# Skip rows made in the output stage from the destination rows, and source rows normalised by ScalarE

## The reference

```
x = layernorm(x + L0(x))      # attention over the edges: 4 heads of 64, then @ W_out
x = layernorm(x + L1(x))

# L1, for z = the normalised row of a node
m   = z @ W_n2m.T                                  # 128 features
q, k, v  = m @ Wq.T + bq, m @ Wk.T + bk, m @ Wv.T + bv
e   = (edge_attr @ W_edge.T) @ We.T
alpha = softmax over the edges of a destination of q[dst] . (k[src] + e) * scale
agg = segment_sum((v[src] + e) * alpha, dst)       # 128 features
x_r = m @ Wskip.T + bskip                          # the skip row
beta = sigmoid([agg, x_r, agg - x_r] @ Wbeta.T)
L1  = (beta * x_r + (1 - beta) * agg) @ W_m2n.T
```

## Time and profile before

| what | us |
|---|---|
| median of 3 runs | 1362.51 (1362.12 to 1378.24) |
| the profiled execution's own time | 1371.76 |
| its span, first to last instruction | 1370.0 |
| mean granted clock of TensorE | 0.958 |

### The profile page before, as it was taken

How to read it: one execution, slowest core, us unless ns; L and a number is a source line. 1 busy time by engine, 2 the same in 40 slices (tenths; PEclk the granted TensorE clock), 3 DMA queues, 4 the chain that set the end, 5 groups by cost and what they waited for, 6 DMA issues and landing times. The chain is left out here.

```text
span 1370.0 us, 28397 instructions
## 1 busy us (share of the span) xinstructions
PE 1198.5 (87%) x7186; PEld 1044.4 (76%) x7186; DVE 1045.4 (76%) x3775; ACT 808.2 (59%) x2683; POOL 838.7 (61%) x1044
## 2 busy tenths in 40 slices
PE   3799999999996799899898699999999994788881
PEld 2688898988895677777776699999999993566660
DVE  3476676776679798889787788888888877788781
ACT  0366565665567765666556466666666667365562
POOL 4688888888743455455444566666666643267675
PEclk9899999999999999999999899999999998799995
DMA  6668889888763487887777766667666642556541
GB/s 157 196 184 260 261 257 273 269 273 266 233 199 121 142 248 237 242 247 240 221 238 208 221 199 196 199 185 211 197 191 204 195 129 78 161 180 185 174 156 57
DMA packets 208937, 277.05 MB, mean 202 GB/s; under 512 B 40060, under 2 KB 140563, under 8 KB 208777
## 3 DMA queue, kind: packets, MB, share of 16 engines
q1 hardware_dynamic: 188793, 224.13, 53.2%
q0 software_dynamic: 19264, 50.85, 12.9%
q10 hardware_dynamic: 720, 0.26, 0.1%
HBM read 159.73 MB, written 117.12 MB: 202 GB/s over the span
## 5 line engine op out<-in xcount | busy, mean ns | idle before, releaser
L743 PE MATMUL banks<-m_ext,node_XT 128*128 128x257 f32 x1568 | 379.9, 385 | 0.0
L743 PEld LDWEIGHTS banks<-m_ext,node_XT 128*128 128x128 f32 x1568 | 288.2, 194 | 33.7
L769 DVE SCALAR_TENSOR_TENSOR node_X<-banks,node_be,node_X 128x256 f32<-128x256 f32 x392 | 169.8, 475 | 83.9 <-ACT node_be L695 69.8
L670 POOL TENSOR_TENSOR node_r<-node_vv,half 128x4 f32<-128x4 f32 (+1 forms) x202 | 214.6, 1062 | 17.2 <-POOL node_vv L665 0.3
L701 ACT ACTIVATE node_XT<-banks 128x512 f32<-128x512 f32 x196 | 117.1, 598 | 143.7 <-PE banks L733 137.5
L665 POOL TENSOR_SCALAR node_vv<-node_mv 128x4 f32<-128x4 f32 (+1 forms) x202 | 57.6, 285 | 223.7 <-DVE node_mv L777 207.2
L762 DVE BATCH_NORM_STATS2 node_st<-node_X 128x6 f32<-128x256 f32 x392 | 145.8, 414 | 17.4 <-DMA node_X<-in_x 16.1
L708 ACT ACTIVATE node_sq<-node_X 128x256 f32<-128x256 f32 x392 | 157.9, 408 | 0.0
L733 PE MATMUL banks<-ident,node_X 128*128 128x128 f32 x784 | 123.6, 281 | 30.1 <-DVE node_X L783 15.1
L682 ACT ACTIVATE node_X<-node_X,node_r 128x256 f32<-128x256 f32 x326 | 145.9, 496 | 1.4 <-POOL node_r L670 1.4
L733 PEld LDWEIGHTS banks<-ident,node_X 128*128 128x128 f32 x784 | 96.7, 150 | 43.0 <-issue 20.1
(11 more groups left out here) (265 smaller groups left out, 2730.6 us busy)
## 6 DMA issues: line engine op xcount, KB each, us to landing
node_X<-in_x SPq DMA_DIRECT2D x196, 256.0 KB
out<-node_X SPq DMA_DIRECT2D x196, 256.0 KB
ring<-rows SPq DMA_DIRECT2D x210, 128.0 KB
rows<-ring SPq DMA_DIRECT2D x100, 256.0 KB
rows<-ring SPq DMA_DIRECT2D x200, 128.0 KB
MB<-keeps SPq DMA_DIRECT2D x40, 320.0 KB, 5.4
store<-rows SPq DMA_DIRECT2D x90, 128.0 KB
MB<-picks SPq DMA_DIRECT2D x50, 128.0 KB
```

Source lines behind the costliest of these rows:

```text
L670: pool.tensor_tensor(r[:, s % 4, NT * lo:NT * hi], v, self.c.half[:, NT * lo:NT * hi], ALU.pow).then_inc(self.roots, 1)
L743: last = pe.matmul(ps[:, NT * o + k, 0:D + 1], self.XT[:, o, k * D + h * P:k * D + (h + 1) * P], c.m_ext[:, h, :], start=(h == 0), stop=(h ...
L769: last = dve.scalar_tensor_tensor(out=X[:, n % U, k, :], in0=ps[:, b + k, 0:D], scalar=self.be[:, n % 4, k:k + 1], in1=X[:, n % U, k, :], ...
```

## The change

Skip rows: the message stage no longer makes or keeps them. In the output stage TensorE transposes the destination rows that are loaded there anyway, in two halves into bank 6; ScalarE copies them with 1.0 added into `ZT` (four slots); two products with `m_ext` give the skip product and its part of the gate's logit (columns 0 to 256). `w_out1` gets two more columns, plus and minus `wa`, so that the aggregate's product carries the other part of the logit in both signs; ScalarE copies these two numbers out (`part`) and gives them as bias to the two sigmoids. The one-column product falls away. The MSG transposes have bank 5 alone, so each waits for the scan of the tile just before. The loads of rows wait for `made` instead of `product`.

Source rows: VectorE normalises the destination side alone. For the source side it makes minus mean times root for two tiles at once (`nb`), in odd steps, as the first instruction of the step, after a wait for `roots`; ScalarE then scales and shifts the row, between its `ST` copy and its K copy. The waits for `normed` of TensorE and GpSimd are joined by waits for `src_normed`; VectorE's QK waits for the Q product itself.

The diff, cut to its core:

```
 Weights, VectorE, s == 1
-                own(dve.tensor_copy(c.wa[:, :], w.wa))
+                own(dve.tensor_copy(c.w_out1[:, D + 1:D + 2], w.wa))
+                own(dve.tensor_scalar(c.w_out1[:, D + 2:D + 3], w.wa, -1.0, None, ALU.mult))
 Message, GpSimd
                 at_least(pool, self.normed, 2 * g - 4)
+                at_least(pool, self.src_normed, 2 * g - 4)
 Message, TensorE
                 pe.wait_ge(self.normed, t + 1)
+                pe.wait_ge(self.src_normed, t + 1)
...
-                at_least(pe, self.x_kept, n)
                 at_least(pe, self.q_used, n)
-                for h in range(2):
-                    pe.matmul(ps[:, 7, DM:2 * DM], c.w_qs[:, h, DM:2 * DM], c.ST[:, o, (2 + h) * P:(3 + h) * P], start=(h == 0), stop=(h == 1))
 Message, ScalarE, after the ST copy
+            if live(t, -1, TILES):
+                n = t + 1
+                g = n // 2
+                k = 2 * (n % 2) + 1
+                act.wait_ge(self.shifted, g + 1)
+                row = c.ring[:, n % c.R, 1, :]
+                act.activation(row, row, ACT.Identity, bias=self.nb[:, g % 3, n % 2:n % 2 + 1], scale=self.r[:, g % 3, k:k + 1]).then_inc(self.src_normed, 1)
...
-                act.wait_ge(self.q_product, n + 1)
-                act.activation(c.store[:, n, DM:2 * DM], ps[:, 7, DM:2 * DM], ACT.Copy).then_inc(self.x_kept, 1)
 Message, VectorE, first in the step
+            if t % 2 == 1 and live(t, -1, TILES):
+                g = (t + 1) // 2
+                dve.wait_ge(self.roots, g + 1)
+                at_least(dve, self.src_normed, 2 * g - 4)
+                dve.scalar_tensor_tensor(out=self.nb[:, g % 3, :], in0=self.mv[:, g % 3, :, 1, 0], scalar=-1.0,
+                                         in1=self.r[:, g % 3, :].rearrange("p (k s) -> p k s", s=2)[:, :, 1], op0=ALU.mult, op1=ALU.mult).then_inc(self.shifted, 1)
...
-                dve.wait_ge(self.x_kept, n + 1)
+                dve.wait_ge(self.q_product, n + 1)
...
-                for side in range(2):
-                    k = 2 * (n % 2) + side
-                    row = c.ring[:, n % R, side, :]
-                    last = dve.tensor_scalar(row, row, self.mv[:, g % 3, n % 2, side, 0:1], self.r[:, g % 3, k:k + 1], ALU.subtract, ALU.mult)
-                last.then_inc(self.normed, 1)
+                row = c.ring[:, n % R, 0, :]
+                dve.tensor_scalar(row, row, self.mv[:, g % 3, n % 2, 0, 0:1], self.r[:, g % 3, 2 * (n % 2):2 * (n % 2) + 1], ALU.subtract, ALU.mult).then_inc(self.normed, 1)
 Output, SP
-                    sp.wait_ge(self.product, n - self.HELD + 1)
+                    sp.wait_ge(self.made, n - self.HELD + 1)
 Output, TensorE, the whole step
             if live(t, 0, TILES):
+                pe.wait_ge(self.rows_in[t % self.M], self.rows_before[t % self.M] + 16 * (t // self.M + 1))
+                at_least(pe, self.zt_ready, t)
+                for h in range(2):
+                    last = pe.transpose(ps[:, 6, h * P:(h + 1) * P], self.row(t)[:, h * P:(h + 1) * P], c.ident[:, :])
+                last.then_inc(self.z_turned, 1)
+            if live(t, 2, TILES):
+                pe.wait_ge(self.zt_ready, n + 1)
+                at_least(pe, self.z_ready, n - 2)
+                for h in range(2):
+                    pe.matmul(ps[:, skip, 0:D + 1], self.ZT[:, n % 4, h * P:(h + 1) * P], c.m_ext[:, h, :], start=(h == 0), stop=(h == 1))
+            if live(t, 0, TILES):
                 pe.wait_ge(self.made, t + 1)
-                at_least(pe, self.scanned, t - 1)
-                pe.transpose(ps[:, 5 + t % 2, 0:P], c.MSG[:, t % G, 0:DM], c.ident[:, :]).then_inc(self.turned, 1)
+                at_least(pe, self.scanned, t)
+                pe.transpose(ps[:, 5, 0:P], c.MSG[:, t % G, 0:DM], c.ident[:, :]).then_inc(self.turned, 1)
             if live(t, 2, TILES):
                 pe.wait_ge(self.scanned, n + 1)
-                pe.matmul(ps[:, skip, 0:D + 1], c.store[:, n, DM:2 * DM], c.w_out1[:, :], start=True, stop=True)
-                pe.matmul(ps[:, skip, D:D + 1], self.AG[:, n % 5, :], c.wa[:, :], start=False, stop=True, skip_group_check=True)
-                pe.matmul(ps[:, agg, 0:D], self.AG[:, n % 5, :], c.w_out1[:, 0:D], start=True, stop=True).then_inc(self.product, 1)
+                pe.matmul(ps[:, self.PAIRS[n % 3][0], 0:D + 3], self.AG[:, n % 5, :], c.w_out1[:, :], start=True, stop=True).then_inc(self.product, 1)
 Output, ScalarE, first in the step
                 act.wait_ge(self.product, n + 1)
+                at_least(act, self.gates_ready, n - 2)
+                act.activation(self.part[:, n % 3, :], ps[:, self.PAIRS[n % 3][0], D + 1:D + 3], ACT.Copy).then_inc(self.parted, 1)
+            if live(t, 0, TILES):
+                act.wait_ge(self.z_turned, t + 1)
+                at_least(act, self.product, t - 3)
+                act.activation(self.ZT[:, t % 4, :], ps[:, 6, 0:D], ACT.Copy, bias=1.0).then_inc(self.zt_ready, 1)
+            if live(t, 3, TILES):
+                n = t - 3
+                act.wait_ge(self.parted, n + 1)
                 at_least(act, self.z_ready, n - 2)
...
-                act.activation(self.gates[:, n % 3, 0:1], logit, ACT.Sigmoid, scale=-1.0)
-                act.activation(self.gates[:, n % 3, 1:2], logit, ACT.Sigmoid).then_inc(self.gates_ready, 1)
+                act.activation(self.gates[:, n % 3, 0:1], logit, ACT.Sigmoid, scale=-1.0, bias=self.part[:, n % 3, 1:2])
+                act.activation(self.gates[:, n % 3, 1:2], logit, ACT.Sigmoid, bias=self.part[:, n % 3, 0:1]).then_inc(self.gates_ready, 1)
```

More of the change, by code:

```diff
@@ L256 @@
     HEADS_READY, NODES_READY, ALL_READY = 1, 2, 3
-    SPREAD, FUSED, MIXED = 19, 24, 27
+    SPREAD, FUSED, MIXED = 20, 25, 28
     def __init__(self, nc, c, ctx):
@@ L305, in emit @@
                 for k in range(2):
-                    pe.matmul(ps[:, 3 + k, 0:D + 1], w.w_skipn[:, k * P:(k + 1) * P], c.w_out1[:, :], start=True, stop=True)
-                pe.matmul(ps[:, 7, 0:D + 1], w.bs_cols, c.w_out1[:, :], start=True, stop=True).then_inc(self.pe_done, 1)
+                    pe.matmul(ps[:, 3 + k, 0:D + 1], w.w_skipn[:, k * P:(k + 1) * P], c.w_out1[:, 0:D + 1], start=True, stop=True)
+                pe.matmul(ps[:, 7, 0:D + 1], w.bs_cols, c.w_out1[:, 0:D + 1], start=True, stop=True).then_inc(self.pe_done, 1)
             if s == 4:
@@ L1273, in __init__ @@
         self.r = sb("r", [P, 3, 4])
+        self.nb = sb("nb", [P, 3, 2])
         self.gathered, self.rows_in, self.kept = c.ring_in, c.ring_load, c.ring_out
@@ L1280, in __init__ @@
         self.attrs = [sem(f"attrs{k}") for k in range(2)]
-        self.padded, self.counted, self.measured, self.widened, self.roots, self.normed, self.a_turned, self.et_ready, self.turned, self.zt_ready, self.q_product, self.kv_product, self.x_kept, self.k_kept, self.v_kept, self.q_used, self.scored = (
-            sem(n) for n in ("padded", "counted", "measured", "widened", "roots", "normed", "a_turned", "et_ready", "turned", "zt_ready", "q_product", "kv_product", "x_kept", "k_kept", "v_kept", "q_used", "scored"))
+        self.padded, self.counted, self.measured, self.widened, self.roots, self.shifted, self.normed, self.src_normed, self.a_turned, self.et_ready, self.turned, self.zt_ready, self.q_product, self.kv_product, self.k_kept, self.v_kept, self.q_used, self.scored = (
+            sem(n) for n in ("padded", "counted", "measured", "widened", "roots", "shifted", "normed", "src_normed", "a_turned", "et_ready", "turned", "zt_ready", "q_product", "kv_product", "k_kept", "v_kept", "q_used", "scored"))
         self.into = c.rows1.rearrange("(t p) d -> t p d", p=P)
@@ L1287, in scored_by @@
         pe.wait_ge(self.v_kept, TILES)
-        pe.wait_ge(self.x_kept, TILES)
     def all_kept(self, eng):
@@ L1510, in __init__ @@
         self.gates = sb("gates", [P, 3, 2])
+        self.part = sb("part", [P, 3, 2])
         self.sq = c.ST[:, :, 0:D]
+        self.ZT = c.AT_flat[:, 0:4 * D].rearrange("p (a n) -> p a n", a=4)
         self.va = sb("va", [P, 3, max(GROUPS)])
@@ L1517, in __init__ @@
         self.keeps = [sem(f"keeps{k}") for k in range(2)]
-        self.made, self.turned, self.scanned, self.gates_ready, self.halfway, self.product, self.z_ready, self.squared, self.widened, self.roots, self.y_ready = (
-            sem(n) for n in ("made", "turned", "scanned", "gates_ready", "halfway", "product", "z_ready", "squared", "widened", "roots", "y_ready"))
+        self.made, self.turned, self.scanned, self.z_turned, self.zt_ready, self.parted, self.gates_ready, self.halfway, self.product, self.z_ready, self.squared, self.widened, self.roots, self.y_ready = (
+            sem(n) for n in ("made", "turned", "scanned", "z_turned", "zt_ready", "parted", "gates_ready", "halfway", "product", "z_ready", "squared", "widened", "roots", "y_ready"))
         self.rows_v = c.rows1.rearrange("(t p) d -> t p d", p=P)
@@ L1635, in emit @@
```

(5 more changed lines are left out.)

6 lines of the change are left out of this document (3 added, 3 removed).

## The result

The changed kernel takes 1412.75 us (median, 1405.38 to 1423.02) against 1362.43 us of the kernel before: 1.0353 times as long, interval 1.0267 to 1.0440. The forecast was 1353. Its profiled execution took 1411.55 us, with a span of 1409.8 us against 1370.0. The kernel before takes 1330 to 1333 us on some occasions and 1361 to 1363 on others, so each experiment is compared with the kernel before as it ran beside it on the same chip. Two executions at a lower mean granted clock, one of the kernel before (1877 us, 0.607) and one of the changed one (1635 us, 0.745), are left out everywhere.

The account below looks back on a forecast made before the run. TensorE was taken to bound the message stage; in the output stage no engine was full, and TensorE would become the limit. Message -24 and output +15 made -9 us: 1353 us for the median, range 1322 to 1384.

Parts of the forecast that it names:

- the costing of the output stage: Output stage: TensorE's work 1.63 us a tile becomes the limit, 1.85 with holds against 1.71 before, +15 us in sum.
- The holds: Output stage: TensorE's word reaches VectorE and ScalarE 1.85 us late, about once in five tiles; forecast loss 1.1 us each.
- rival C: Output stage: the hold adds whole to TensorE's 1.63, giving 2.0 us a tile, +33 us, 1372 in all; chance 0.20.
- The message stage: Message stage: 0.44 gained less 0.15 and 0.05 lost, 0.24 us a tile, 24 us gained.
- the skip matmuls: Message stage: TensorE loses two skip-row matmuls, 0.44 us a tile, 44 us over 100 tiles as upper bound.
- The wait for the roots: Message stage: VectorE's bias waits for GpSimd's roots at the head of odd steps, ahead of V; 0.15 us a tile.
- ScalarE's longer step: Message stage: ScalarE's added source norm mostly covered by matmuls; 0.05 us a tile charged for late ST copies after node steps.
- The rule of the Trainium skill: Source norm moved to ScalarE: by the rule 0.17 us a tile, 17 us lost; forecast charged nothing, ScalarE being idle enough.
- A: Whole kernel, the forecast itself: message stage -24 us, output stage +15 us, 1353 us; chance 0.45.
- B: Both stages: the new waits are absorbed, message -38 us, output 0, 1324 us; chance 0.20.
- D: Message stage: each free gap pays the full 1.28 us, leaving 2 us gain, 1376 us in all; chance 0.15.
- marks of being wrong at the root: Holds vanish or grow with the new order, other engines wait for ScalarE, or kept rows land after their transposes want them.

Follow-up runs that it names:

- e1: The changed kernel with TensorE's MSG transpose moved ahead of the skip product in the output step; 1327.16 us, 0.9954 of the kernel before.
- e8: The kernel before run once more, unchanged, beside e5 and e7; 1326.65 us in one execution.
- e9: e1 with the source norm's bias made at the end of VectorE's odd steps instead of the head; 1354.49 us, 0.9955 of the kernel before.
- e12: The kernel of e5 run again on another occasion; 1349.01 us against 1362.94 for the kernel before, 0.9896.
- e5: The changed kernel with both norms on VectorE as before and the MSG transpose ahead of the skip product; 1313.56 us, 0.9869 of the kernel before.
- e10: e1 with ScalarE's source norm moved behind its K copy instead of ahead of it; 1382.60 us, 1.0158 of the kernel before.
- e6: e5 plus only a wait for GpSimd's roots at the head of VectorE's odd message steps; 1327.22 us, 0.9974 of the kernel before.
- e4: The changed kernel with both sides normalised on VectorE as before, so only the skip rows are moved; 1374.35 us, 1.0306 of the kernel before.
- e7: The changed kernel run once more, unchanged, as reference beside e5 and e6; 1387.95 us, 1.0423 of the kernel before.
- e2: The changed kernel with VectorE's second addition moved ahead of its scan in the output step; 1328.69 us, 0.9973 of the kernel before.
- e11: The changed kernel with the second half of the skip product left out, queue order as changed; 1367.56 us against 1361.07, one execution.

## Why the prediction was wrong

**The failed step** is the costing of the output stage: "So TensorE becomes the limit, and the question is what the holds do." I summed each engine's work and took the largest, 1.63. The sum was right: with the ring cut, TensorE's tile is 1.636 (e1) where 1.63 stood. But I had listed TensorE's new order and not asked what each wait in it now stands ahead of. The skip product's wait for `z_ready` was moved past the MSG transpose, and I priced no wait for it. I even credited TensorE with doing "the skip product, the MSG transpose and the aggregate" during a hold. The ring could have been summed from the kernel before: 0.87 for the skip product as forecast, 0.27 for the transpose, and from the order of time shown above 1250.85 - 1250.45 = 0.40, 0.46 and some 0.2 of waking (1251.46 - 1251.31 = 0.15 of it): 2.2 us a tile, an estimate. That is 0.5 above the old 1.71, or some 50 us, and would have turned the sign. Measured in place of the forecast 1.85: a ring of 2.26 us, with holds 2.38, and 68 us over 100 tiles.

**The holds** were taken for a fixed part of the program. They come and go with the occasion: in e1 to e8 there is none, whichever order the kernel has; in e9 to e12 each has them. Their place, though, belongs to the program. In the profile after and in those of e9 and e12 alike, a long gap stands before scan 34, 39, 44 and so on (counted from 0), the last of each five tiles whose factors are loaded together; in the profile before it is mostly the scan after that. In the profile after, the ring's own slack hides most of one. VectorE then loses 0.6 us in five tiles (mean 2.38 less median 2.26), not 1.85. With the ring cut and holds present they cost 1.951 - 1.636 = 0.31 a tile (e12, and the same in e9 and e10), 1.6 us for five tiles. I had said 1.1; here too the size was off, towards rival C.

**The message stage** was nearly right in sum: 24 us forecast, 21 measured between the K/V products. By terms: the skip matmuls gave 0.34 a tile (e5, 3.61 to 3.27), not the 0.44 of their duration. In e5 TensorE is idle for 3.0 of 250 us there (0.4 before), 0.03 a tile more, and VectorE is 94% busy. Where the rest goes I can't divide further. The wait for the roots cost 0.15 when it alone was added (e6 against e5) and 0.09 when it was taken away (e9 against e1), forecast 0.15. The whole move of the norm cost 0.14 (e1 against e5), so for ScalarE's longer step, charged with 0.05, the runs leave something between nothing and 0.05. The gain was put 0.10 too high and the losses 0.06 too high, which gave 0.24 against 0.20 or 0.21 measured: part of the agreement is luck. As forecast, VectorE waits for the roots in about every third or fourth tile, and its waits after, 800 to 1090 us, say so:

```profile
DVE message_nb L1441 <- POOL message_r L1320: 27.9, 25, 1.2
```

25 waits in 290/3.41 = 85 tiles, 1.1 us each. That is 0.33 us of VectorE a tile, and less than half of it reaches TensorE. The rule of the Trainium skill that I had weighed ("ScalarE: Activation LUTs", section "Rules for kernel authors": multiply and add on VectorE) comes out right for this kernel: undoing the move gives 0.13 us a tile (e4 against e7). But most of it is another price than the operation's: 0.09 to 0.15 us of it is the early wait that the bias needs.

**The rivals.** A's message part held, its output part did not. B (waits absorbed) is refuted by e6: the wait costs 13.7 us. C named the stage and the sign, and its mark, a tile over 1.95, was met, but its mechanism was not the cause: its 2.0 a tile is what e12 shows for holds without the ring (1.95), while the changed kernel had 2.38. D (each gap pays in full) is refuted: about 0.15 a tile, not 0.37. Of what I had named as marks of being wrong at the root, the first ("if the holds vanished or grew") was again about holds; ScalarE was not what paced the stage (e1, e2); and only the first two tiles' transposes waited for their rows, 2.96 and 1.90 us in the profile after. The mark that came true, VectorE's scan waiting for a transpose that ended just before, stood in no list.

## What to carry to other kernels

When a reordering puts an instruction with a wait ahead of one that had none, follow the wait round: who releases it, what stands before the releaser in its own queue, and whether that needs the instruction now queued behind. If it does, the sum along that ring is a lower bound of the step, whatever the shares of the engines. An operation that costs nothing under cover can still need an input earlier than anyone did before; price the wait, not the operation. In this profile, several engines at 50 to 80% with a steady tile and waits in a circle were the sign of such a ring, and one swap of queue order is worth trying before any work is cut.

## What the runs showed of the hardware that was not expected

- The engines that wait for TensorE can start late on one occasion and not on another, with the same kernel at the same granted clock (1.00) and, by its number, on the same chip (e5 and e12). In e11 the transpose had ended at 1253.42 by the profile, whose ends for TensorE are modelled; the scan that waits for it started 1.65 later:

```profile
1253.15 0.27 PE L1597 MATMUL banks<-ident,MSG 128*128 128x128 f32 x1
...
1255.07 0.48 DVE L1664 TENSOR_TENSOR_SCAN S<-MB,S,banks 128x128 f32<-128x128 f32 x1 [1.98 <-remote]
```

  Where it comes, it comes about once in five tiles, at the same tiles of the group, and in the output stage. Whether the work itself or the word of its end is late, and why, stays open; no experiment here settled it. The message stage of e12 (3.272 us a tile) is the same as that of e5 (3.269).
- A sigmoid of one column takes 0.17 us in the kernel before and 255 to 263 ns in the changed one, where it has a column as its bias. Two of these a tile add some 0.2 us of busy time to ScalarE's step, which e1 shows at 97.27/61 = 1.59 us a tile (61 tiles in 100 us) where I had said about 1.5.

```profile
L1623 ACT ACTIVATE output_gates<-banks,output_part 128x1 f32<-128x1 f32 x64 | 16.9, 263 | 0.0
L1622 ACT ACTIVATE output_gates<-banks,output_part 128x1 f32<-128x1 f32 x64 | 16.3, 255 | 0.0
```
